# Which six weight tiles stay resident, and where one down tile stands in the last stages

## The chip, the cores and the metric

The kernel runs on one core of one Trainium2 chip. The metric is the device time of one execution in microseconds; three runs of the kernel before gave 2692.3, 2694.03 and 2695.58, with a median of 2694.03.

## The reference

Four sequences of 1024 tokens, 512 wide, go through two blocks, each of the form x = x + layernorm(block(layernorm(x))), all in float32.

```
proj = x @ W_in + b_in;  hidden, gate = split(proj)          # 512 -> 2 x 1024
conv = silu(causal depthwise conv of 4 taps (hidden))
dt_in, B, C = split(conv @ W_x);  delta = softplus(dt_in @ W_dt + b_dt)
h = exp(delta * A) * h + delta * conv * B;  y = sum_n h * C   # 16 states, over the tokens
block 1 = ((y + conv * d_param) * silu(gate)) @ W_out + b_out

x = fwht(x * SU_ug) / 64                                      # Hadamard transforms,
up, g = x @ W_up.T * s, x @ W_gate.T * s                      # folded into the weights by the kernel
block 2 = (fwht(silu(g) * up * SU_dp) / 64) @ W_down.T * s    # 512 -> 2048 -> 512
```

## The kernel before

The 4096 tokens are cut into NCH = 16 chunks of T = 256. The work is a pipeline of stages c = 0 to 18; each stage has 32 slots k. In stage c the scan runs for chunk c (`cur`), the input projection and the convolution for chunk c + 1 (`front`), the output projection of block 1 for chunk c - 1 (`back`), the feed-forward for chunk c - 2 (`ff`) and its remainder for chunk c - 3 (`fold`). Stages 16, 17 and 18 have no `cur` and no `front`: in stage 16 `back` is chunk 15, `ff` 14 and `fold` 13; in stage 17 `ff` is 15 and `fold` 14; in stage 18 only `fold` 15 is left. Each engine's instructions are written out slot by slot by its own function `slot`, and the engines meet in semaphores only.

The feed-forward of a chunk has HT = 16 tiles of 128 hidden units; tile ft of chunk j is number no = 16 j + ft. Each tile is `up_gate` (L686, 24 matmuls of 128x256: weights and activations are split into a high and a low part, three passes over each), then tanh on ScalarE, two products on VectorE, the split of the product into `prod_hi` (ScalarE) and `prod_lo` (GpSimd, `low`, L1356 on), and `down` (L707, 6 matmuls of 128x512, which add up in the two banks pD). In a stage, `up_gate(ff, ft)` stands in slot 2 + 2 ft and `down(ff, ft)` in slot 7 + 2 ft, up to ft = 12; down 13 and up_gate 15 stand in slot 0 of the next stage, down 14 in its slot 3, down 15 in its slot 5. In slot 1 `turn_f` transposes the feed-forward input of the next chunk into the bank hT; ScalarE and VectorE split it into fxT_hi and fxT_lo (`f_hi`, `f_low`), for which `up_gate(ff, 0)` waits. `turn_h` and `turn_y`, the transposes of the scan's last states and its sum, take the same bank after it. From chunk 14 on odd tiles use the bank `decay` in place of `pF`, as the scan is over.

The weights of one tile (1 MB for up and gate, `wug`; 0.5 MB for down, `wd`) are read again for each chunk into a ring of two buffers each. All DMAs are issued by SyncE in one program order. `load_ug` (L388) of a ring tile waits until the up_gate two ring tiles earlier is done, `load_wd` (L404) until the down two ring tiles earlier is. In slot k (odd) SyncE comes to the up and gate weights of tile (k + 1)/2, in slot k (even) to the down weights of tile (k - 4)/2; in slot 18, ahead of the down weights, `store_out` (L441) waits for the finished output of chunk c - 3, and in slot 20 `load_res` reads the residual rows.

When the scan is over its buffers hold six resident tiles, `kept_ug` and `kept_wd`: those of `KEPT` (L57). They are read once, in chunk 14 (`free_kept` waits until the scan's buffers are free), and used for chunks 14 and 15; `kept(no)` (L227) says which tile is resident, and `RINGED` numbers the others.

Of the kernel before, what the change touches and what calls it, by code (L numbers as in the profile page):

```python
# [19 lines left out]
NCH = TOK // T  # L20
# [6 lines left out]
def wait_first(eng, sem, value, passed):  # L27

    eng.wait_ge(sem, value)
    eng.sem_inc(passed, 1)  # L30


HT = FF // P


def fused_block(nc, x, W, scratch_bc, scratch_ug, scratch_wd, out):
# [17 lines left out]
        had_in1 = first("had_in1", [P, KT, DM])  # L54
        had_in2 = first("had_in2", [P, KT, DM])
    had_in = (had_in0, had_in1, had_in2)
    KEPT = range(2, 8)  # L57
    kept_ug, kept_wd = {}, {}
    with ExitStack() as once:
        once.enter_context(nc.sbuf_tensor("tail_pad0", [P, 8 * KT * T + 7 * T + 3 * TB * DM + TB * DI + DT * DM], F32))  # L60
# [7 lines left out]
    with ctx:  # L68
# [118 lines left out]
        for c in range(LAST + 1):  # L187
            cur, front, back, ff = chunk(c), chunk(c + 1), chunk(c - 1), chunk(c - 2)
# [38 lines left out]
        def kept(no):  # L227

            j, ft = divmod(no, HT)
            return ft - KEPT.start if j >= NCH - 2 and ft in KEPT else None  # L230

        RINGED = [no for no in range(NCH * HT) if kept(no) is None]
        RING_NO = {no: i for i, no in enumerate(RINGED)}
# [131 lines left out]
        def _(sp):  # L365
# [14 lines left out]
            def free_kept(i):  # L380

                wait_first(sp, y_gated, NCH - 1, sp_passed)
                if i in (1, 2, 3):
                    wait_first(sp, scan_done, NQ * NST * NCH, sp_passed)
                if i in (4, 5):
                    wait_first(sp, h_turned, TB * NST * NCH, sp_passed)

            def load_ug(j, ft):  # L388
                no = j * HT + ft
                if kept(no) is not None:  # L390
                    if j == NCH - 2:
                        free_kept(kept(no))
                        sp.dma_start(kept_ug[kept(no)][:, :, :, :].bitcast(F32), scratch_ug[ft, :, :, :].rearrange("p s (k m) -> p s k m", k=KT)
                                     ).then_inc(ug_kept[kept(no)], 16)
                    return
                i = RING_NO[no]
                if i >= 2:
                    wait_first(sp, ug_mm, RINGED[i - 2] + 1, sp_passed)
                if no == 0:
                    for part in ("r_hi", "r_lo"):  # L400
                        wait_first(sp, had_stored[part], 16 * SETS.count("r"), sp_passed)
                sp.dma_start(wug[i % 2][:, :, :, :].bitcast(F32), scratch_ug[ft, :, :, :].rearrange("p s (k m) -> p s k m", k=KT)).then_inc(ug_in[i % 2], 16)

            def load_wd(j, ft):  # L404
                no = j * HT + ft
                if kept(no) is not None:
                    if j == NCH - 2:
                        free_kept(kept(no))
                        sp.dma_start(kept_wd[kept(no)][:, :, :].bitcast(F32), scratch_wd[ft, :, :, :]).then_inc(wd_kept[kept(no)], 16)
                    return  # L410
                i = RING_NO[no]
                if i >= 2:
                    wait_first(sp, down_mm, RINGED[i - 2] + 1, sp_passed)
                if no == 0:
                    wait_first(sp, had_mm, NTILE, sp_passed)
                sp.dma_start(wd[i % 2][:, :, :].bitcast(F32), scratch_wd[ft, :, :, :]).then_inc(wd_in[i % 2], 16)
# [129 lines left out]
        def _(pe):  # L546
# [40 lines left out]
            def turn_f(j):  # L587
                pe.wait_ge(fn_done, TB * (j + 1))
                begin_t(("f", j, 0))
                for kt in range(KT):  # L590
                    for tb in range(TB):
                        mm = pe.transpose(hT[:, kt * T + tb * P:kt * T + (tb + 1) * P], ob[:, tb, kt * P:(kt + 1) * P], ident[:, :])
                mm.then_inc(fx_turned, 1)
# [92 lines left out]
            def up_gate(j, ft):  # L686
                no = j * HT + ft
                if kept(no) is None:
                    pe.wait_ge(ug_in[RING_NO[no] % 2], 16 * (RING_NO[no] // 2 + 1))
                else:  # L690
                    pe.wait_ge(ug_kept[kept(no)], 16)
                if ft == 0:
                    pe.wait_ge(fx_lo, 2 * (j + 1))
                if no:
                    pe.wait_ge(p_done, bank_users(no))
                else:
                    pe.wait_ge(had_lo, NTILE)
                if no == SPARE + 1:
                    pe.wait_ge(scan_done, NQ * NST * NCH)
                for which in (1, 0):  # L700
                    for kt in range(KT):
                        for i, (a, b) in enumerate(PASSES):
                            mm = pe.matmul(gate_up_bank(no)[:, which, :], ug_tile(no)[:, 2 * which + a, kt, :], fxT[b][:, kt, :],  # L703
                                           start=(kt == 0 and i == 0), stop=(kt == KT - 1 and i == len(PASSES) - 1))
                mm.then_inc(ug_mm, 1)

            def down(j, ft):  # L707
                no = j * HT + ft
                if kept(no) is None:
                    pe.wait_ge(wd_in[RING_NO[no] % 2], 16 * (RING_NO[no] // 2 + 1))  # L710
                else:
                    pe.wait_ge(wd_kept[kept(no)], 16)
                pe.wait_ge(p_lo, no + 1)
                if ft == 0 and j:
                    pe.wait_ge(z_evac, TB * j)
                split = (prod_hi[no % 2], prod_lo[no % 2])
                for tb in range(TB):
                    for i, (a, b) in enumerate(PASSES):
                        mm = pe.matmul(pD[tb][:, :], split[a][:, tb * P:(tb + 1) * P], wd_tile(no)[:, b, :],  # L719
                                       start=(ft == 0 and i == 0), stop=(ft == HT - 1 and i == len(PASSES) - 1))  # L720
                mm.then_inc(down_mm, 1)
# [27 lines left out]
            def in_slot(c, k, cur, front, back, ff, fold):  # L749
                n, tb = divmod(k, 2)  # L750
                if k == 0:
                    if front is not None:
                        turn_x(front)
                    if fold is not None:
                        down(fold, HT - 3)
                    if back is not None:
                        turn_h(back, NST - 1, 0)
                    if fold is not None:
                        up_gate(fold, HT - 1)
                    return  # L760
                if k == 1:
                    if ff is not None:
                        turn_f(ff)
                    if front is not None:
                        in_proj("hid", front, *PE_HID[0])
                    if back is not None:
                        turn_h(back, NST - 1, 1)
                    if front is not None:
                        in_proj("hid", front, *PE_HID[1])
                    return  # L770
                if k in (2, 3):
                    if back is not None:
                        turn_y(back, k - 2)
                    if ff is not None and k == 2:
                        up_gate(ff, 0)
                    if front is not None and k == 3:
                        in_proj("hid", front, *PE_HID[3])
                    if cur is not None:
                        turn_h(cur, 0, tb)
                    if front is not None and k == 2:  # L780
                        in_proj("hid", front, *PE_HID[2])
                    if fold is not None and k == 3:
                        down(fold, HT - 2)
                    return
                if cur is not None:
                    turn_h(cur, n - 1, tb)
                if ff is not None and k in UG_SLOT:
                    up_gate(ff, UG_SLOT[k])
                if front is not None and k in PE_HID:
                    in_proj("hid", front, *PE_HID[k])  # L790
                if back is not None:
                    out_proj(back, PE_OUT.get(k, ()))
                if cur is not None and k in PE_GATE:
                    in_proj("gate", cur, *PE_GATE[k])
                if front is not None:
                    x_proj(front, PE_XPROJ.get(k, ()))
                if ff is not None and k in DOWN_SLOT:
                    down(ff, DOWN_SLOT[k])
                if fold is not None and k in DOWN_LATE:
                    down(fold, DOWN_LATE[k])  # L800
                if front is not None:
                    if k == 23:
                        turn_rows(front)
                    if k in PE_DT:
                        dt_proj(front, PE_DT[k])
# [679 lines left out]
```

## Time and profile before

| | |
|---|---|
| median of three runs | 2694.03 us |
| the profiled execution, its own time | 2690.62 us |
| its span | 2688.8 us |
| TensorE busy | 2584.6 us (96%) |
| VectorE busy | 2239.1 us (83%) |
| GpSimd busy | 2046.8 us (76%) |
| ScalarE busy | 1818.1 us (68%) |
| DMA, mean over the span | 210 GB/s |

Times in the views are microseconds from the start of the span. Stage 16 begins at about 2493, stage 17 at about 2591, stage 18 at about 2669. In the view by stretches a line has the stretch, its length, then for PE, PEld, DVE, ACT and POOL the busy time and in brackets the count, then the granted clock (1.00 is 2.4 GHz), the DMA share and GB/s. In the chain of waits each line is start, duration, and what the chain ran through. "issue" is time in which the engine waited for nothing that the profile shows. L602, L610 and L592 are the transposes of turn_y, turn_h and turn_f, L703 is up_gate, L719 is down.

### The profile page before, as it was taken

Reading aid. Unit: us, or ns where it says so; the run is one execution under the profiler, and the core shown is the slowest. Engines: PE = TensorE matmul, PEld = TensorE weight load, DVE = VectorE, ACT = ScalarE, POOL = GpSimd, SP = SyncE. Lnnn points to the kernel's source line nnn. Section 1 sums busy time; section 2 is a strip of 40 time slices with the busy share of each in tenths; the row PEclk is TensorE's granted clock in tenths of the full one; section 3 lists DMA queues with packets and bytes.
Section 4 is the critical chain, followed back from the end, with each engine's and each line's share of the span. In section 5 each row is a group of like instructions: output and inputs, shape, how many; then the busy total and the mean of one; then the engine's idle time right before and its main releaser. Section 6 shows DMA issues by size and latency. Waiting matters only on the chain.

```text
span 2688.8 us, 46296 instructions
## 1 busy us (share of the span) xinstructions
PE 2584.6 (96%) x16048; PEld 2191.9 (82%) x16048; DVE 2239.1 (83%) x2567; ACT 1818.1 (68%) x3939; POOL 2046.8 (76%) x1692
## 2 busy tenths in 40 slices
PE   7899889999999999999999999999999999989987
PEld 5566568989888888988888888988888888878786
DVE  6698799898889889898889889898889888889321
ACT  4576677777777777777777777777777777755221
POOL 6576779788797979888797979888797979766222
PEclk9999999999999999999999999999999999999999
DMA  5554245766666665766666665766666665656564
GB/s 179 192 187 155 104 160 200 235 208 228 220 222 222 218 221 199 240 212 225 220 225 224 215 221 201 236 210 231 220 226 217 220 214 200 216 188 227 227 258 173
DMA packets 165193, 564.41 MB, mean 210 GB/s; under 512 B 17248, under 2 KB 19680, under 8 KB 132960
## 3 DMA queue, kind: packets, MB, share of 16 engines
q1 hardware_dynamic: 164960, 561.44, 60.5%
q8 instruction: 129, 2.11, 0.3%
q14 instruction: 104, 0.85, 0.1%
HBM read 527.30 MB, written 34.08 MB: 209 GB/s over the span
## 4 chain that ended last, share of the span: by engine, by line
PE 77%; DVE 10%; ACT 7%; issue 3%; DMA 2%; POOL 1%; SPq 0%; POOLq 0%; DVEq 0%; ACTq 0%
PE pF L703 21%; PE hT L610 13%; PE pM L628 13%; PE pD L719 10%; PE pM L680 8%; DVE h L1131 5%; DVE acc L1144 3%; PE pD L740 3%; PE pM L650 3%; PE decay L703 2%; PE hT L602 1%; ACT decay L952 1%; PE pF L740 1%; ACT delta L929 1%; ACT delta L924 1%
## 5 line engine op out<-in xcount | busy, mean ns | idle before, releaser
L1131 DVE TENSOR_TENSOR_SCAN h<-decay,dbx 128x512 f32<-128x512 f32 x1024 | 1201.2, 1206 | 97.6 <-ACT decay L952 68.1
L1299 POOL TENSOR_TENSOR dbx<-u,bb 128x2048 f32<-128x2048 f32 (+1 forms) x272 | 1179.1, 4335 | 37.7 <-DVE h L1131 35.7
L952 ACT ACTIVATE decay<-delta,a_neg 128x255 f32<-128x255 f32 x2048 | 875.5, 468 | 309.4 <-DVE h L1131 302.3
L703 PE MATMUL pF<-fxT_hi,wug 128*128 128x256 f32 x3744 | 735.2, 289 | 6.6 <-DMA wug<-scratch_ug 4.5
L1144 DVE SCALAR_TENSOR_TENSOR acc<-hT,bcT,acc 128x1024 f32<-128x1024 f32 x480 | 609.7, 1270 | 126.8 <-PE hT L610 123.4
L703 PEld LDWEIGHTS pF<-fxT_hi,wug 128*128 128x128 f32 x3744 | 604.1, 193 | 8.3 <-DMA wug<-scratch_ug 5.8
L610 PEld LDWEIGHTS hT<-ident,h 128*128 128x128 f32 x4096 | 472.3, 141 | 150.0 <-issue 96.9
L610 PE MATMUL hT<-ident,h 128*128 128x128 f32 x4096 | 534.6, 274 | 34.9 <-DVE acc L1144 22.5
L703 PE MATMUL pF<-fxT_lo,wug 128*128 128x256 f32 x1872 | 531.9, 284 | 0.0
L628 PE MATMUL pM<-xnT,w_in 128*128 128x256 f32 x2016 | 480.5, 381 | 10.6 <-ACT hid L872 4.9
L628 PEld LDWEIGHTS pM<-xnT,w_in 128*128 128x128 f32 x2016 | 366.2, 191 | 56.2 <-ACT hid L872 6.5
L1363 POOL TENSOR_TENSOR prod_lo<-prod,prod_hi 128x256 fp32r<-128x256 f32 x256 | 187.2, 731 | 293.0 <-ACT prod_hi L983 292.3
L703 PEld LDWEIGHTS pF<-fxT_lo,wug 128*128 128x128 f32 x1872 | 361.8, 193 | 0.2
L719 PE MATMUL pD<-wd,prod_hi 128*128 128x512 f32 x976 | 351.6, 441 | 3.8 <-POOL prod_lo L1363 2.0
L1356 POOL TENSOR_TENSOR conv<-conv,tap 128x256 f32<-128x256 f32 x360 | 261.3, 731 | 30.8 <-ACT tap L898 12.0
L680 PE MATMUL pM<-w_out,gate 128*128 128x512 f32 x512 | 240.4, 593 | 4.3 <-ACT hid L872 2.3
L719 PEld LDWEIGHTS pD<-wd,prod_hi 128*128 128x128 f32 x976 | 177.1, 190 | 59.6 <-issue 30.0
L719 PE MATMUL pD<-wd,prod_lo 128*128 128x512 f32 x488 | 192.8, 395 | 0.0
L976 ACT ACTIVATE th<-pF,half_gate 128x256 f32<-128x256 f32 x240 | 111.9, 466 | 107.1 <-PE pF L703 104.9
L898 ACT ACTIVATE tap<-hid,taps 128x256 f32<-128x256 f32 x360 | 155.6, 497 | 0.0
L1285 POOL COPY carry<-h 128x8 f32<-128x8 f32 x192 | 36.9, 192 | 149.3 <-issue 96.2
L1166 DVE SCALAR_TENSOR_TENSOR prod<-th,pF 128x256 f32<-128x256 f32 x240 | 98.7, 411 | 58.5 <-ACT th L976 58.5
(170 smaller groups left out, 2711.5 us busy)
## 6 DMA issues: line engine op xcount, KB each, us to landing
wug<-scratch_ug SPq DMA_DIRECT2D x244, 1024.0 KB, 4.8
wd<-scratch_wd SPq DMA_DIRECT2D x244, 512.0 KB, 4.0
w_in<-in_W_in SPq DMA_DIRECT2D x252, 256.0 KB, 2.9
bb<-scratch_bc SPq DMA_DIRECT2D x128, 256.0 KB, 4.7
xb<-in_hidden_states SPq DMA_DIRECT2D x16, 512.0 KB, 4.8
xr<-in_hidden_states SPq DMA_DIRECT2D x16, 512.0 KB, 6.0
out<-xr SPq DMA_DIRECT2D x16, 512.0 KB, 3.7
kept_ug<-scratch_ug SPq DMA_DIRECT2D x6, 1024.0 KB, 9.1
```

Of the source, the lines that this page charges most:

```text
L610: mm = pe.transpose(hT[:, dt * P:(dt + 1) * P], h[n % 2][:, dt, tb * P:(tb + 1) * P], ident[:, :])
L628: mm = pe.matmul(pM[:, a, :], w[:, kt, :], xnT[j % 2][:, kt, :], start=(kt == 0), stop=(kt == KT - 1))
L680: mm = pe.matmul(o, gate[:, dt, tb * P:(tb + 1) * P], w_out[:, dt, :], start=(dt == 0), stop=(dt == DT - 1))
L703: mm = pe.matmul(gate_up_bank(no)[:, which, :], ug_tile(no)[:, 2 * which + a, kt, :], fxT[b][:, kt, :], start=(kt == 0 and i == 0), stop=( ...
L719: mm = pe.matmul(pD[tb][:, :], split[a][:, tb * P:(tb + 1) * P], wd_tile(no)[:, b, :], start=(ft == 0 and i == 0), stop=(ft == HT - 1 and ...
L898: e = act.activation(tap[dt % 2][:, k, :], hid[:, dt, k:k + T], ACT.Copy, scale=taps[:, dt, k:k + 1])
L952: e = act.activation(da[q % 2][:, i, 1:], delta[c % 2][:, dt, 1:], ACT.Exp, scale=a_neg[:, dt, n:n + 1])
L1131: dve.tensor_tensor_scan(row(h[n % 2][:, tiles, :]), row(da[q % 2][:, :, :]), row(dbx[n % 2][:, tiles, :]), 0.0, ALU.mult, ALU.add).then_i ...
L1144: dve.scalar_tensor_tensor(acc[c % 2][:, tb, :], hT[:, :], cn, acc[c % 2][:, tb, :], ALU.mult, ALU.add).then_inc(acc_done, 1)
L1299: pool.tensor_tensor(dbx[n % 2][:, tiles, :], u[:, tiles, :], rows, ALU.mult).then_inc(done if restarts(c) else prod_done, 1)
L1356: pool.tensor_tensor(conv[j % 2][:, dt, :], conv[j % 2][:, dt, :], tap[dt % 2][:, k, :], ALU.add).then_inc(tap_added, 1)
L1363: pool.tensor_tensor(prod_lo[no % 2][:, :], prod[no % 2][:, :], prod_hi[no % 2][:, :].bitcast(F32), ALU.subtract).then_inc(p_lo, 1)
```

## The change

The resident tiles are 2, 4, 6, 8, 10 and 12 in place of 2 to 7. Tile 14 of chunk 15 is also read into a resident place, that of tile 2, after tile 2 of chunk 15 has been used (`second_use`); the semaphores of that place then count to 32. In stages without `cur` (16, 17, 18), `down(fold, 14)` is written out in slot 1, behind `turn_f`, in place of slot 3.

```
-    KEPT = range(2, 8)
+    KEPT = (2, 4, 6, 8, 10, 12)
         def kept(no):
             j, ft = divmod(no, HT)
-            return ft - KEPT.start if j >= NCH - 2 and ft in KEPT else None
+            if j >= NCH - 2 and ft in KEPT:
+                return KEPT.index(ft)
+            return 0 if second_use(no) else None
+
+        def second_use(no):
+            return no == HT * NCH - 2
+
+        FIRST_USE = HT * (NCH - 1) + KEPT[0]
             def load_ug(j, ft):
                 no = j * HT + ft
                 if kept(no) is not None:
-                    if j == NCH - 2:
+                    if second_use(no):
+                        wait_first(sp, ug_mm, FIRST_USE + 1, sp_passed)
+                    elif j == NCH - 2:
                         free_kept(kept(no))
+                    if second_use(no) or j == NCH - 2:
                         sp.dma_start(kept_ug[kept(no)] ...).then_inc(ug_kept[kept(no)], 16)
                     return
...
-                    pe.wait_ge(ug_kept[kept(no)], 16)
+                    pe.wait_ge(ug_kept[kept(no)], 32 if second_use(no) else 16)
...
                 if k == 1:
                     if ff is not None:
                         turn_f(ff)
+                    if cur is None and fold is not None:
+                        down(fold, HT - 2)
                     if front is not None:
                         in_proj("hid", front, *PE_HID[0])
...
-                    if fold is not None and k == 3:
+                    if cur is not None and fold is not None and k == 3:
                         down(fold, HT - 2)
```

`load_wd` and the wait in `down` change in the same way as `load_ug` and the wait in `up_gate`, with `down_mm` and `wd_kept`.

## Rows read from the trace of the kernel before

**Rows 1.** The page, busy time of TensorE, its share and its instructions.

```profile
PE 2584.6 (96%) x16048; PEld 2191.9 (82%) x16048; DVE 2239.1 (83%) x2567; ACT 1818.1 (68%) x3939; POOL 2046.8 (76%) x1692
```

**Rows 2.** Stretches of 5 us: five engines' busy time, granted clock, DMA share, GB/s.

```profile
2500.00:2505.00 5.00, 2.84 (x17) 2.64 (x18) 2.67 (x5) 0.58 (x2) 0.58 (x1) 0.75 1.02 429
2505.00:2510.00 5.00, 5.00 (x28) 5.00 (x28) 1.66 (x4) 0.04 (x1) 0.14 (x1) 0.57 0.13 54
...
2530.00:2535.00 5.00, 5.00 (x22) 3.01 (x21) 1.01 (x3) 0.47 (x1) 0.00 (x0) 1.00 1.03 425
...
2645.00:2650.00 5.00, 4.79 (x33) 4.14 (x32) 1.12 (x3) 0.89 (x2) 0.73 (x1) 1.00 0.88 329
```

**Rows 3.** Chain of waits, start of stage 16: start, duration, what it ran through.

```profile
2500.69 1.11 PE hT L610 x8
...
2503.25 1.94 PE hT L602 x8
2505.19 4.73 PE pF L703 x24
...
2510.80 1.38 PE pD L719 x6
```

**Rows 4.** TensorE in order of time, behind turn_f of stage 16; brackets: idle before.

```profile
2500.69 0.33 PE L610 MATMUL hT<-ident,h 128*128 128x128 f32 x1 [2.01 <-DVE fxT_lo L1158]
```

**Rows 5.** GpSimd in order of time: the low halves for the two moved down tiles.

```profile
2493.27 0.73 POOL L1363 TENSOR_TENSOR prod_lo<-prod,prod_hi 128x256 fp32r<-128x256 f32 x1 [5.65 <-ACT prod_hi L983]
...
2590.28 0.72 POOL L1363 TENSOR_TENSOR prod_lo<-prod,prod_hi 128x256 fp32r<-128x256 f32 x1 [5.40 <-ACT prod_hi L983]
```

**Rows 6.** Chain of waits, late stage 16 and early stage 17.

```profile
2559.97 2.89 PE decay L703 x24
...
2562.94 7.52 DMA wug<-scratch_ug
...
2583.64 7.52 DMA wd<-scratch_wd
...
2592.86 2.87 PE decay L703 x24
...
2596.60 2.06 issue
2598.66 3.11 PE pF L703 x24
...
2603.16 2.87 PE decay L703 x24
...
2607.42 2.87 PE pF L703 x24
```

**Rows 7.** SyncE in order of time: issues at the ends of its two long waits.

```profile
2522.58 0.42 SPq L402 DMA_DIRECT2D wug<-scratch_ug  x1
2555.25 0.39 SPq L444 DMA_DIRECT2D out<-xr  x1
...
2632.80 0.39 SPq L444 DMA_DIRECT2D out<-xr  x1
```

**Rows 8.** DMA issues at 2595.82, 2498.32 and 2522.58: count, KB each, us to landing.

```profile
wug<-scratch_ug SPq DMA_DIRECT2D x1, 1024.0 KB, 4.7
...
wd<-scratch_wd SPq DMA_DIRECT2D x1, 512.0 KB, 5.5
...
wug<-scratch_ug SPq DMA_DIRECT2D x1, 1024.0 KB, 20.8
```

**Rows 9.** Chain of waits, last tiles of stage 17.

```profile
2641.50 2.89 PE pF L703 x24
...
2654.56 7.60 DMA wug<-scratch_ug
...
2662.21 4.63 PE pF L703 x24
...
2669.59 2.89 PE decay L703 x24
```

More of the change, by code:

```diff
@@ L406, in load_wd @@
                 if kept(no) is not None:
-                    if j == NCH - 2:
+                    if second_use(no):
+                        wait_first(sp, down_mm, FIRST_USE + 1, sp_passed)
+                    elif j == NCH - 2:
                         free_kept(kept(no))
+                    if second_use(no) or j == NCH - 2:
                         sp.dma_start(kept_wd[kept(no)][:, :, :].bitcast(F32), scratch_wd[ft, :, :, :]).then_inc(wd_kept[kept(no)], 16)
@@ L711, in down @@
                 else:
-                    pe.wait_ge(wd_kept[kept(no)], 16)
+                    pe.wait_ge(wd_kept[kept(no)], 32 if second_use(no) else 16)
                 pe.wait_ge(p_lo, no + 1)
```

## The prediction

> **What bounds the kernel now.** I read the page first: TensorE is busy 96% of the span [rows 1], so only TensorE's own order and its idle time are worth anything, and the diff touches work in the last two hundred microseconds alone. There I read the stretches of 5 us, then the chain of waits, then SyncE's issues. The chain has three places for the reader.
>
> *The start of stage 16.* turn_f(14) ends at 2498.7, and TensorE then stands idle 2.01 us until VectorE has read the bank hT [rows 4]; another gap comes before turn_y, which starts at 2503.25 [rows 3]. TensorE is at its upper level (2.4 GHz) before, at 0.75 in 2500 to 2505 and at 0.57 in 2505 to 2510 [rows 2]: it fell to 1.2 GHz behind two gaps with one group of transposes between. The first feed-forward group there takes 4.73 us [rows 3] where the others take 2.87 [rows 6].
>
> *The late half of stage 16 and the last tiles of stage 17.* Here the chain runs through DMAs: up_gate(14,11) waits for a wug load, down(14,13) for a wd load, each 7.52 us after its issue [rows 6]; at the end a load of 7.60 us and a group of 4.63 [rows 9]. In the undisturbed part a tile (an up_gate and a down) comes every 4.26 us (2607.42 less 2603.16), of which up_gate is 2.87 and so down 1.39 [rows 6]. From up_gate(14,9) to up_gate(14,15) the chain takes 2592.86 - 2559.97 = 32.89 us; without waits it would be 5 x 4.26 + 2.87 + 2 x 1.39 = 26.95. **5.9 us are lost there.** From up_gate(15,10) to up_gate(15,15) it takes 2669.59 - 2641.50 = 28.09, without waits 4 x 4.26 + 5.65 = 22.69. **5.4 us are lost there**, 1.8 of them in the group of 4.63 us at half clock [rows 9].
>
> *Why the loads are late.* In a run of ring tiles, load i is issued when up_gate i-2 is done, so two tiles take a landing plus one up_gate: 7.5 + 2.9 = 10.4 us against the 8.5 that TensorE needs. A lone load lands in 4.7 us [rows 8]; it takes 7.5 because a wd load and the next wug load share the engines. And SyncE issues nothing between 2522.58 and 2555.25 and waits again before 2632.80 [rows 7]: both are the store of the feed-forward output, which sits in program order in slot 18.
>
> **The change part by part.**
>
> *down(f,14) behind turn_f, in stages 16 and 17.* Six matmuls, 1.39 us, move from the TensorE path (2510.80 in the chain, 1.38 [rows 3]) into the idle time behind turn_f: 2.01 us in stage 16 [rows 4], 2.06 in stage 17 [rows 6]. In stage 16 its low half is subtracted at 2493.27 to 2494.0 and in stage 17 at 2590.28 to 2591.0 [rows 5], before turn_f ends. Its weights in stage 16 are asked for before that, by a wait that the change leaves. It ends 0.6 us before hT comes free, so turn_h behind it is not delayed; if cover failed it would cost its 1.39 again, no more. The next in line at the old place, up_gate(.,1), waits for product 13,15 or 14,15, which VectorE has by then, as a whole up_gate(.,0) lies between. Nothing is queued behind the new wait that another engine needs sooner, and SyncE's load wd(14,0) is freed earlier. Gain 1.4 + 1.4 = **2.8 us**. In stage 18 the order is the old one, since turn_f is missing there and down(15,14) isn't moved ahead of anything.
>
> *The clock at 2502.* With down(13,14) in the first gap, TensorE has matmuls until 2500.1, idles 0.6, turns h, idles 1.5. At half clock turn_y cost 1.94 - 1.11 = 0.83 more and up_gate(14,0) 4.73 - 2.87 = 1.86 more [rows 3, 6]: 2.7 together. Bounds: 0 (it falls anyway) and 2.7, or a little more, as the gap of 2.06 at 2596.6 is filled too, where this profile had no fall but another execution may have. The nearest row is that one: a single gap of 2.06 between matmuls and 3.11 for the group behind it, not 4.73 [rows 6]. After the change the stretch is milder still. I take **2.7 us**.
>
> *Every other tile, stage 17.* Before, tiles 8 to 15 of chunk 15 come through the ring one after another; after, ring tiles are 0, 1, 3, 5, ... 13 and 15, so a ring load is issued two tiles and more ahead, some 10 us before its use against a landing of 4.7 to 7.6. Tile 14 is read into the place of tile 2, whose up_gate ends at 2610.3 [rows 6]; its load stands in order behind the loads of tile 13 and wd 11, issued some 12 us before up_gate(15,14). wd(15,15) waits for down(15,11), about 12 us ahead. After the store at 2632.80 the first down that needs a new load, down(15,7), is 7 us away, as before. So all of the **5.4 us** go, and with them the half clock at 2662, which stood behind a wait for a load. What is late next is nothing of the DMA: the closing chain tanh, product, high, low, down(15,15) stays.
>
> *Every other tile, stage 16.* Up to slot 18 SyncE issues the same loads as before (wug to tile 9, wd to tile 6), a few of them later: wug(14,3) now waits for up_gate(14,0), done 9 us before it is needed, wug 7 for up_gate 3, wug 9 for up_gate 5. These have slack, since out_proj stands between. After slot 18, wug 10, wd 8, wug 11, wd 9, wug 12 and wd 10 are now issued at once, not one by one. So the ring's round trip is gone and what bounds is the rate. From the store's issue (1.4 earlier than 2555.25) I lay the transfers behind one another in units of 512 KB: store, wd 7, wug 10 (2 units), residual, wd 8, wug 11, wd 9, wug 12, wd 10, wug 13, wd 11, wug 14, wd 12. Rate from the burst, 425 GB/s in 2530 to 2535 [rows 2], is 1.23 us a unit; from a ring stretch, 329 GB/s in 2645 to 2650, 1.59. The first lands some 3 us after its issue, an estimate below the 4.7 of a lone load of twice the size [rows 8].
> At 1.23 each tile lands before its use (wug 11 at about 2566 against 2566.9, wug 12 at 2570 against 2571, wug 13 at 2574 against 2575, wug 14 at 2578 against 2580). One wait is left: wd(14,13) is issued behind wug(14,15), which waits for up_gate(14,13). From there to down(14,13) are 1.39 + 2.87 + 1.39 = 5.65 us, and the pair needs 0.1 + 0.4 + 5.5 [rows 8], with 0.2 for the start: 0.6 late.
> At 1.59 the lateness is 1.1 at wug 11, about 0.5 at each of 12, 13 and 14, and 2.1 at wd 13: 4.7 in all.
> So the gain is between 5.9 - 4.7 = 1.2 and 5.9 - 0.6 = 5.3. The queue is deep here as in the burst, whose last load lands 20.8 us after issue for 16 units ahead of it [rows 8], so I stay near the fast end: 1.6 left, **4.3 us** gained.
>
> The Trainium skill (DMA: Bandwidth & Descriptors, Specifications) gives a core about 358 GB/s from HBM and 435 for the fabric. By the first figure a unit takes 1.47 us, an estimate, and the stage would keep some 2.2 us of waits; by the second it is my fast end. The trace has 425 GB/s of loads for 5 us [rows 2], so it doesn't agree with the first as a ceiling.
>
> **Sum.** 2.8 + 2.7 + 5.4 + 4.3 = 15.2 us. The profiled execution took 2690.62 (span 2688.8 and 1.8 around it), 3.4 below the median 2694.03. 2690.6 - 15.2 = 2675.4; against the median **2678.8 us**. From these four terms alone the time is 2675.0 to 2681 (1.0 more in stage 16 and one more fall of the clock spared, 1.8, at the low end).
>
> **The rivals.**
>
> *A. The clock falls all the same behind turn_f of stage 16.* For: between 2500.1 and 2504 there is still only a group of transposes between two gaps. Against: less idle than now, and no fall at 2596.6. All else holds: 12.5 gained, 2681.5.
>
> *B. The rate bounds stage 16.* For: the 329 GB/s, and the ring loads' landings don't follow the burst's pace. Against: with six transfers queued it is the burst's state. 2.8 + 1.2 + 5.4 with or without the clock: 9.4 to 12.1, 2682 to 2684.6.
>
> *C. It doesn't do what it says.* wd(14,14), which down(14,14) now needs at turn_f's end, is issued behind wug(15,0), 0.5 us behind the end of up_gate(14,14), and from there to turn_f's end are some 6.7 us. If both lag at the slow rate it is 3 late, the whole of stage 17 shifts by it, and with B little but the last 5.4 is left: 9.4 - 3 - 1.4 = 5, 2689. For: before, it landed as turn_f ended. Against: its own wait is now for down(14,11), not 12.
>
> *D. Slower, by the clock.* Place: any group after turn_f in stages 16 or 17. If TensorE fell to 1.2 GHz and stayed there, each up_gate costs 1.86 more and each down 1.4 more, 3.3 a tile. It decides from four tiles in a row (12.5 / 3.3); seven would give 2704. For: two falls in this stretch. Against: none outlasts two groups, all stand behind gaps, and the change only takes gaps away.
>
> **Chances.** Forecast 0.55, A 0.23, B 0.14, C 0.05, D 0.03. The range is from 2675.0 to 2684.6, which holds the forecast's case, A and nearly all of B. This kernel's measurement tells 0.2% (5.4 us) from no change. The forecast, A and B are faster by more: 0.92. C lies at the bound: 0.05 within. D: 0.03 slower.
>
> **What would show it.** In the trace after: down with wd directly behind the transposition of ob and TensorE idle some 0.6 before the next; the granted clock at 2500 to 2510 whole; from tile 9 of chunk 14 on a tile every 4.26 us, with one wait below 1 us at down(14,13); no DMA wait in stage 17 and no group over 3.2 us; wug issues at six within 6 us of the store. I am wrong if waits for wug of tiles 11 to 14 sum to over 3 us, if the moved down waits for its weights, or if the gain is under 9 us.

## The result, and the profile after

The changed kernel takes **2677.09 us** (median of six, 2674.68 to 2677.48) against 2692.61 for the kernel before (median of six, 2689.90 to 2695.58), 15.5 less. The ratio is 0.9942, 95% interval 0.9930 to 0.9954. The forecast was 2678.8, with a range of 2675.0 to 2684.6.

The profiled execution took 2677.31 (span 2675.5) against 2690.62. Its line numbers are shifted: turn_f is L606, turn_y L616, turn_h L624, up_gate L717, down L733.

The chain of waits at the start of stage 16, to be laid beside [rows 3]:

```profile
2501.30 1.11 PE hT L624 x8
...
2503.86 1.06 PE hT L616 x8
2504.93 2.88 PE pF L717 x24
2507.80 0.87 PE hT L616 x8
2508.68 2.88 PE decay L717 x24
2511.55 1.39 PE pD L733 x6
2512.94 2.87 PE pF L717 x24
```

turn_y takes 1.06 in place of 1.94 and up_gate(14,0) 2.88 in place of 4.73; the down between turn_y and up_gate(14,1) is gone. The stretches of 5 us, with the granted clock in the third column from the end, against [rows 2]:

```profile
2500.00:2505.00 5.00, 2.91 (x21) 2.22 (x21) 3.31 (x6) 1.19 (x3) 0.00 (x0) 1.00 0.96 401
2505.00:2510.00 5.00, 5.00 (x45) 5.00 (x44) 2.91 (x8) 2.13 (x3) 0.74 (x1) 1.00 0.73 254
```

TensorE's idle times from there to stage 17, in order of time (idle before and its end in brackets), against [rows 4]:

```profile
2501.30 1.09 PE L624 MATMUL hT<-ident,h 128*128 128x128 f32 x8 [0.62 <-DVE fxT_lo L1174]
...
2564.04 0.73 PE L733 MATMUL pD<-kept_wd,prod_hi 128*128 128x512 f32 x2 [0.43 <-DMA kept_wd<-scratch_wd]
...
2566.54 0.39 PE L717 MATMUL decay<-fxT_hi,wug 128*128 128x256 f32 x1 [0.83 <-DMA wug<-scratch_ug]
...
2584.72 0.73 PE L733 MATMUL pD<-wd,prod_hi 128*128 128x512 f32 x2 [0.87 <-DMA wd<-scratch_wd]
...
2592.17 0.36 PE L717 MATMUL pF<-fxT_hi,wug 128*128 128x256 f32 x1 [0.41 <-issue]
```

The chain from late stage 16 to the end, which answers to [rows 6, 9]:

```profile
2578.72 5.95 DMA wd<-scratch_wd
...
2584.72 1.66 PE pD L733 x6
2586.38 2.86 PE decay L717 x24
2589.24 0.87 PE hT L606 x8
2590.11 1.65 PE pD L733 x6
2591.76 0.41 issue
2592.17 3.11 PE pF L717 x24
2595.28 2.88 PE decay L717 x24
...
2599.55 2.87 PE pF L717 x24
...
2656.29 2.89 PE decay L717 x24
```

No DMA stands in stage 17 any more: from up_gate(15,2) at 2599.55 to up_gate(15,15) at 2656.29 there are 56.74 us, against 62.17 before (2607.42 to 2669.59). The loads have their lead: the last one for the ring, wug(15,15), is issued at 2640.85 and lands at 2645.4, 10.9 us ahead of its use; before it was issued at 2658.89 and landed at 2666.2, 3.4 us ahead, and wug(15,14) landed at 2662.2 for a group that starts at 2662.21.

**Where the time of the two profiles went.** Four pieces are bounded by instructions that all kernels have: the twelve matmuls of down(13,12) and down(13,13), up_gate(14,2), up_gate(14,15), up_gate(15,2), up_gate(15,15), the end. All traces of the study, in us; the pieces are read from the chain of waits, and in no_second_use and early_store, where the chain passes by a bound, from TensorE in order of time:

| trace | to up(14,2) | to up(14,15) | to up(15,2) | to up(15,15) | from the first to the end |
|---|---|---|---|---|---|
| before | 25.15 | 76.43 | 14.56 | 62.17 | 197.52 |
| before_again_a | 24.98 | 75.01 | 16.01 | 64.90 | 200.41 |
| before_again_b | 24.98 | 74.96 | 16.02 | 61.35 | 196.54 |
| after | 21.05 | 73.44 | 13.17 | 56.74 | 183.61 |
| changed_again | 21.05 | 72.19 | 13.16 | 56.75 | 182.39 |
| changed_third | 21.04 | 72.98 | 13.18 | 56.74 | 183.17 |
| down_only | 21.03 | 75.76 | 13.20 | 62.99 | 192.97 |
| tiles_only | 24.97 | 73.10 | 14.57 | 56.74 | 188.61 |
| gap_filled | 22.78 | 75.01 | 14.90 | 62.85 | 194.83 |
| no_second_use | 21.04 | 72.38 | 13.16 | 57.48 | 183.27 |
| residual_later | 21.03 | 72.21 | 13.19 | 56.74 | 182.41 |
| early_store | 21.03 | 71.31 | 13.19 | 56.74 | 181.55 |
| early_store_wd_first | 21.03 | 70.46 | 13.18 | 56.74 | 180.68 |
| best_again | 21.03 | 70.46 | 13.19 | 56.74 | 180.64 |

The mean from there to the end is 198.16 for the three traces of before and 183.06 for the three of the changed kernel: 15.1 less. What lies ahead is the same work in all and yet not the same time: the twelve matmuls start between 2488.19 and 2493.89. A single pair of spans is worth no more than that. The pieces agree far better, apart from the fourth in the kernel before, which goes from 61.35 to 64.90.

### The profile page after: what moved, and what is told of

It is laid out like the page before. It is cut to its first block, busy times and chain, and to the rows that moved or that the text cites. A ratio compares the mean times of both kernels' runs of the same rounds, so it can differ in the third digit from the quotient of the medians.

```text
span 2675.5 us, 46296 instructions
## 1 busy us (share of the span) xinstructions
PE 2581.3 (96%) x16048; PEld 2190.1 (82%) x16048; DVE 2238.6 (84%) x2567; ACT 1818.1 (68%) x3939; POOL 2046.8 (77%) x1692
## 4 chain that ended last, share of the span: by engine, by line
PE 77%; DVE 10%; ACT 8%; issue 3%; DMA 1%; POOL 1%; SPq 0%; POOLq 0%; DVEq 0%; ACTq 0%
PE pF L717 21%; PE hT L624 14%; PE pM L642 13%; PE pD L733 10%; PE pM L694 8%; DVE h L1147 5%; DVE acc L1160 3%; PE pD L754 3%; PE pM L664 3%; PE decay L717 2%; ACT decay L968 1%; PE hT L616 1%; PE pF L754 1%; ACT delta L945 1%; ACT delta L940 1%
## 5 line engine op out<-in xcount | busy, mean ns | idle before, releaser
L717 PE MATMUL pF<-fxT_hi,wug 128*128 128x256 f32 x3632 | 710.2, 289 | 0.4 <-issue 0.4
L624 PEld LDWEIGHTS hT<-ident,h 128*128 128x128 f32 x4096 | 472.8, 141 | 148.5 <-issue 96.7
L717 PEld LDWEIGHTS pF<-fxT_hi,wug 128*128 128x128 f32 x3632 | 583.6, 192 | 0.9 <-issue 0.8
L624 PE MATMUL hT<-ident,h 128*128 128x128 f32 x4096 | 535.2, 274 | 33.6 <-DVE acc L1160 22.5
L717 PE MATMUL pF<-fxT_lo,wug 128*128 128x256 f32 x1816 | 514.8, 283 | 0.0
L733 PE MATMUL pD<-wd,prod_hi 128*128 128x512 f32 x972 | 350.8, 442 | 2.8 <-POOL prod_lo L1379 2.0
L717 PEld LDWEIGHTS pF<-fxT_lo,wug 128*128 128x128 f32 x1816 | 349.8, 193 | 0.0
L733 PEld LDWEIGHTS pD<-wd,prod_hi 128*128 128x128 f32 x972 | 176.7, 190 | 58.9 <-issue 30.5
L733 PE MATMUL pD<-wd,prod_lo 128*128 128x512 f32 x486 | 192.0, 395 | 0.0
L694 PEld LDWEIGHTS pM<-w_out,gate 128*128 128x128 f32 x512 | 88.3, 191 | 67.8 <-issue 63.1
```

The costliest lines, as they stand in the source:

```text
L624: mm = pe.transpose(hT[:, dt * P:(dt + 1) * P], h[n % 2][:, dt, tb * P:(tb + 1) * P], ident[:, :])
L694: mm = pe.matmul(o, gate[:, dt, tb * P:(tb + 1) * P], w_out[:, dt, :], start=(dt == 0), stop=(dt == DT - 1))
```

## The experiments

All were timed beside the kernel before on their chip, whose medians were 2691.3 (24 executions, first four kernels), 2689.0 (9, next four) and 2689.8 (9, last four).

**down_only**: the moved down alone.

```
     KEPT = range(2, 8)                      # as before
+                    if cur is None and fold is not None:
+                        down(fold, HT - 2)  # slot 1, behind turn_f
```

> Only the moved down tile (13,14 and 14,14 behind turn_f); resident tiles 2 to 7 as before. Theory: it gives 2 x 1.4 us of TensorE time and 2.7 us of spared half clock at the start of stage 16, so 5.5 us below the kernel before; the waits for ring loads in late stage 16 (5.9 us) and stage 17 (5.4 us) stay, since each ring load is issued by TensorE's own progress and so shifts with it. Rival 1 (the clock at 2502 is a matter of the execution, not of the filled gap): 2.8 us. Rival 2 (the ring stretches swallow what is gained ahead of them): under 2 us.

Median 2686.10, ratio 0.9979 (0.9970 to 0.9988), so 5.2 us by the medians, as the theory has it. The first piece is 4.1 us shorter, the third 1.4. Both rivals fall: without the clock the first piece would have stayed at 23.6 to 23.8, and the stretches of the ring swallow nothing that the traces could tell: they have 75.76 and 62.99, within what the three traces of before show. Stage 17 keeps its waits.

**tiles_only**: the alternating tiles alone.

```
     KEPT = (2, 4, 6, 8, 10, 12)             # as in the changed kernel
-                    if cur is None and fold is not None:
-                        down(fold, HT - 2)
-                    if cur is not None and fold is not None and k == 3:
+                    if fold is not None and k == 3:
                         down(fold, HT - 2)
```

> Only the alternating resident tiles and the second use of tile 2's place; the down tile stays in slot 3. Theory: stage 17 gives 5.4 us, late stage 16 some 3.0 as in the changed kernel, so 8.4 us below the kernel before, 5.5 above the changed kernel; the half clock at the start of stage 16 stays. Rival (the parts help each other: with the down in its old place the loads behind the store of slot 18 are relatively earlier or later): stage 16 differs from the changed kernel by more than 1 us.

Median 2682.11, ratio 0.9971 (0.9960 to 0.9981), 9.2 us by the medians. Stage 17 has its 56.74, late stage 16 lies among the changed kernel's three (73.10), and the first piece and the third are those of before, with the half clock. The two gains add up to 14.4 by the medians, against the 15.5 of the whole change; by the traces' last column they are 5.2 and 9.6, 14.7 together, against 15.1. So the parts don't help or hinder each other by more than about 1 us, which is as fine as these runs can tell.

**no_second_use**: tile 14 of chunk 15 in the ring.

```
         def second_use(no):
-            return no == HT * NCH - 2
+            return False
```

> The changed kernel with tile 14 of chunk 15 in the ring instead of in tile 2's place. Theory: the second use is worth nothing: wug(15,15) would wait for up_gate(15,13), from whose end to up_gate(15,15) there are 1.39 + 2.87 + 1.39 + 1.39 = 7.0 us against a landing of 4.7 to 6, so within 0.5 us of the changed kernel. Rival (three ring tiles in a row at the end are enough for a late load, as the traces before show landings of 7.5 us): 1 to 3 us slower than the changed kernel, with a wait for wug or wd in the last 12 us of TensorE.

Median 2674.97, ratio 0.9948 (0.9935 to 0.9961): not told apart from the changed kernel. The trace shows the small wait that the theory denied, TensorE in order of time:

```profile
2653.44 0.73 PE L733 MATMUL pD<-wd,prod_hi 128*128 128x512 f32 x2 [0.45 <-DMA wd<-scratch_wd]
```

It is down(15,13), late behind its load by 0.45, 0.7 with the slower start, and stage 17 has 57.48 us in the table against 56.74. So the second use, with most of the diff's lines, brings 0.7 us of the 15 in this one trace: more than the 0.5 of the theory, less than the rival's 1 to 3.

**gap_filled**: nothing moved, the gap filled with idle work.

```
                     if ff is not None:
                         turn_f(ff)
+                    if c == LAST - 2:
+                        spare = da[1][:, :, :].rearrange("p a t -> p (a t)")
+                        for _ in range(3):
+                            pe.matmul(spare, ident[:, :], w_out[:, 0, :], start=True, stop=True)
```

> The kernel before with three 128x512 matmuls of constant data, whose result nobody reads, behind turn_f of stage 16; nothing is moved. They take some 1.3 us of the 2.0 us gap. Theory (the gap lets the clock fall, filling it keeps it up): the clock stays whole from 2500 to 2510, up_gate(14,0) takes 2.9 us, gain 2.7 us. Rival 1 (the fall is chance): fall in the profile and a gain within 0.5 us of zero. Rival 2 (the fall only moves to another place): no gain, with half clock elsewhere in stage 16.

Median 2688.50, 2.8 below the kernel before by the medians, but the ratio is 0.9995 (0.9986 to 1.0004), which allows for no gain as well as for the 2.7 expected: the executions alone don't decide it. The chain of waits does:

```profile
2499.19 0.87 PE hT L592 x8
2500.06 2.58 PE decay L767 x6
2502.64 0.89 PE hT L610 x8
...
2504.99 1.06 PE hT L602 x8
2506.05 2.88 PE pF L703 x24
```

The spare matmuls took 2.58 us, not the 1.3 expected, and held turn_h back by some 0.6. Even so the first piece is 22.78 against 24.97 to 25.15 in the four traces with the empty gap: 2.2 to 2.4 won with work that computes nothing. turn_y and up_gate(14,0) have the times of full clock, and there is no half clock in the rest of stage 16. Rivals 1 and 2 fell, as far as one trace can tell; the traces that follow say the same of rival 1.

**before_again_a**, **before_again_b**: the kernel before, for its trace.

> The kernel before once more, for its trace. Theory (the empty 2.0 us behind turn_f of stage 16 bring the clock down): half clock from about 2502 to 2509 again, up_gate(14,0) at 4.5 us or more, as in the two traces with the empty gap so far, against none of the seven traces where the gap is filled. Rival (chance): full clock there. The part up to stage 16 will differ by up to 2.5 us from the first trace, with the places of half clock before 400 us.

> As before_again_a. Half clock near 2502 again. The fall at 2662 is expected only if the waits for wug at tiles 13 and 14 of chunk 15 fall as in the first trace; over the traces the length from stage 16's start to the end is 196 to 199 us.

One execution each, 2696.11 and 2692.21 us. Half clock is there both times (stretches of before_again_a, the granted clock third from the end):

```profile
2500.00:2505.00 5.00, 2.38 (x20) 1.90 (x18) 1.86 (x3) 1.45 (x3) 0.00 (x0) 0.97 0.63 235
2505.00:2510.00 5.00, 4.14 (x20) 4.17 (x21) 3.12 (x7) 0.42 (x1) 0.72 (x1) 0.50 0.69 289
2595.00:2600.00 5.00, 2.94 (x26) 2.74 (x25) 1.69 (x4) 1.45 (x3) 0.00 (x0) 1.00 0.64 217
2600.00:2605.00 5.00, 5.00 (x28) 4.86 (x27) 0.55 (x2) 0.89 (x2) 0.73 (x1) 0.66 0.42 175
```

So it fell in all four traces with the empty gap of stage 16 (before three times, tiles_only) and in none of the ten with the filled one (eight when the expectation above was written, not seven). The last row was not expected: it falls behind turn_f of stage 17 too, where [rows 6] show 3.11 for the same up_gate(15,0). The chain of before_again_a there:

```profile
2599.67 4.60 PE pF L703 x24
```

before_again_b has the same 4.60. The third piece is 16.0 there, not 14.6: what the moved down saves in stage 17 is then 1.4 and 1.45 of clock. before_again_a had a fall at 2671 as well and 64.90 us in stage 17. Its length to the end, 200.41, lies outside the 196 to 199 expected. But the same gap of 2.06 behind turn_f of stage 17 is also in tiles_only and gap_filled, and there the clock held: it fell in two of five traces with that gap empty, and in none of the nine in which the moved down fills it.

**changed_again**, **changed_third**: the changed kernel itself.

> The changed kernel itself, beside the next three on one chip. It should stand 13.3 to 15.5 us below the kernel before, with 2.9 to 3.0 us of waits and restarts left between up_gate(14,9) and up_gate(14,15).

> The changed kernel, third trace, beside the next kernel: from the two downs ahead of stage 16 to the end 182.4 to 183.6 us, as in the two traces so far; 1.7 to 3.0 us of it waits for loads in stage 16.

Medians 2677.06 and 2676.34, ratios 0.9951 (0.9937 to 0.9966) and 0.9941 (0.9929 to 0.9954). By the medians that is 11.9 and 13.5 below the kernel before on the same chip, against 15.5 in the result: the first lies under the 13.3 expected, and the nine executions of before beside it spread over 10.6 us. Above the 70.46 that up_gate(14,2) to up_gate(14,15) takes without any wait, the three traces have 3.0, 1.7 (changed_again, where 2.9 to 3.0 were expected) and 2.5.

**residual_later**: the residual rows behind wug(14,11).

```
-                if k == 20 and back is not None:
+                if k == 20 and cur is not None and back is not None:
                     load_res(back)
...
                         load_ug(j, ft % HT)
+                    if k == 21 and cur is None and back is not None:
+                        load_res(back)
```

> The changed kernel with the residual rows of chunk 15 asked for behind wug(14,11) (slot 21) in place of ahead of wd(14,8) (slot 20), in stage 16 and after alone. Theory (the waits of 0.4 us at down(14,8) and 0.8 at up_gate(14,11) are the residual's place in the queue: it and the 2.9 us until the next landing, where others take 1.3): both waits vanish, about 1.7 us faster than the changed kernel with their restarts, and the slow landing stands behind wug 11. Rival (the slow landing belongs to the start of the burst behind the store, whatever comes first): wd 8 is still late, gain at most 0.8 us.

Median 2676.18, ratio 0.9947 (0.9932 to 0.9962), 0.9 below the changed kernel on the same chip: no gain that the times can tell. The waits at down(14,8) and up_gate(14,11) are gone, but the piece is 72.21 as against 72.19 in changed_again, since down(14,13) waits longer, TensorE in order of time:

```profile
2579.78 0.73 PE L735 MATMUL pD<-wd,prod_hi 128*128 128x512 f32 x2 [1.13 <-DMA wd<-scratch_wd]
```

That wait is 0.87, 0.64 and 1.25 in the three traces of the changed kernel, so its length here may be chance. And my reason falls: with nothing of the residual ahead of it, wug(14,11) still landed 3.5 us after its forerunner (2560.4 against 2556.9) where two units take 2.5. The slow landing comes within the first transfers behind the store, whichever they are. The rival has that right, but not that wd 8 would still be late.

**early_store**: the data of the store are ready earlier.

```
                 if n == 9:
...
-                    if fold is not None:
+                    if fold is not None and cur is not None:
                         add_z(fold)
+                if n == 6 and fold is not None and cur is None:
+                    add_z(fold)
```

> The changed kernel with GpSimd's addition of the feed-forward output to the residual (add_z) in slot 12 in place of slot 18, in stages without scan; SyncE's store of slot 18 then finds its data ready. Theory (SyncE stands behind the store for no need; the memory moves 0 GB/s from 2540 to 2550): the store and the loads behind it go out some 15 us earlier, no wait for wug or wd is left but that of down(14,13), some 1.8 us faster than the changed kernel. Rival (the late half is bound by the rate): waits at tiles 11 to 14 stay.

Median 2674.95, ratio 0.9945 (0.9929 to 0.9962). The store goes out at 2535.73 in place of 2551.76, and a tile comes every 4.26 us from 2547.71 on. What waits is down(14,13), 0.56 us, and, 0.20, the moved down(14,14). It is 2.1 us below the changed kernel by the medians and 1.5 by the last column of the table, against 1.8 expected. The rate did not bind: the rival fell. The early store was not tried on the kernel before, so what it would have done for the ring loads without the alternating tiles isn't known.

**early_store_wd_first** and **best_again**: also the last two loads of stage 16 exchanged.

```
+                    if c == NCH and k == 29:
+                        load_wd(j, HT - 3)
                     if j is not None:
                         load_ug(j, ft % HT)
...
-                    if j is not None:
+                    if j is not None and not (c == NCH and k == 30):
                         load_wd(j, ft % HT)
```

> early_store and, in stage 16, wd(14,13) asked for ahead of wug(14,15), for which SyncE waits until up_gate(14,13) is done. Theory (the remaining 0.9 us wait, 1.1 with its restart, is that order alone): the wait at down(14,13) goes, no DMA is left in the chain of stage 16, 2.9 us faster than the changed kernel. Rival (wug(14,15) becomes late in its place): a wait of 0.5 to 1 us at up_gate(14,15), and no more than early_store brings.

> early_store_wd_first again. Theory: no DMA in the chain from stage 16 on, the same 180.7 us from there to the end, 1.7 to 2.9 below the changed kernel of this call; in the time of the executions 2 us, at the edge of what the runs can tell. Rival (the first trace was a lucky one): a wait for wug or wd returns.

Medians 2674.86 and 2674.41, ratios 0.9943 (0.9929 to 0.9957) and 0.9937 (0.9923 to 0.9950). No DMA stands in the chain from stage 16 on. Late stage 16 of best_again:

```profile
2577.83 2.87 PE pF L719 x24
2580.71 2.75 PE pD L735 x12
2583.45 2.87 PE decay L719 x24
```

down(14,12) and down(14,13) run as twelve matmuls without a gap, and up_gate(14,15) follows. The two traces take 180.68 and 180.64 to the end, 2.4 below the changed kernel's mean. The medians lie 2.2 and 1.9 below the changed kernel's on the same chips; the intervals of the ratios overlap, so the trace shows this gain and the times only agree with it.

## Why the prediction was right

*The moved down, 2.8.* Right. Six matmuls stand behind turn_f, idle 0.62 is left in stage 16 and 0.41 in stage 17, up_gate(14,1) directly follows turn_y, and the third piece is 1.4 shorter. Its weights in stage 17 came at the last moment: issued at 2582.98 and 7.1 us on the way, they landed at 2590.1, as turn_f ended. The gap behind it hid the slow start (1.65 for 1.39). That was rival C's place, and the margin was as thin as I feared: in early_store and no_second_use this down waited for its weights by 0.20 and 0.22.

*The clock at 2502, 2.7.* Right in place and size. First piece: 4.0 shorter, of which 1.39 is the down, so 2.6 for the clock. gap_filled shows it apart from any moved work. Rival A gets none of ten traces. What I held against it, that a single gap of 2.06 leaves the clock whole at 2596.6 [rows 6], holds only in part: it did so in three of five traces, and the other two fell.

*Stage 17, 5.4.* Right, 5.43 between these traces; from the other two traces of before it is 8.2 and 4.6, so the fit of the one number owes something to the trace it was worked out from. But the second use of tile 2's place, to which I gave a paragraph, has 0.7 of it; the alternation does the rest.

*Late stage 16, 4.3, with 1.6 us of waits left.* **This term was mis-sized.** The profiles have 73.44 against 76.43, 3.0 gained; over three traces of each, 72.9 against 75.5, 2.6 gained and 2.4 left. The wait at down(14,13), forecast 0.6 with its start, was 0.87 and its 0.26, of the kind foreseen: early_store keeps it and the exchange of the two loads removes it. The step that was off is "one wait is left": there are three in this trace, 0.43 at down(14,8), 0.83 at up_gate(14,11) and that one. The first two come from the landings at the front of the queue. DMA issues of the changed kernel at 2551.76, 2556.17 and 2570.28 (count, KB each, us to landing):

```profile
out<-xr SPq DMA_DIRECT2D x1, 512.0 KB, 3.3
...
wug<-scratch_ug SPq DMA_DIRECT2D x1, 1024.0 KB, 10.3
...
kept_wd<-scratch_wd SPq DMA_DIRECT2D x1, 512.0 KB, 8.7
```

From the store's landing at 2555.1 to wug(14,11)'s at 2566.5 seven units of 512 KB came in 11.4 us, 1.63 each; from there to wd(14,12)'s at 2579.0 ten in 12.5, 1.25 each. I had taken 1.23 for all of them. So the landings of the first tiles came at the slow end of my bounds (1.59) and the rest at the fast one, which is why the waits are at tile 8 and tile 11 and nowhere behind. But the reason that I gave for the slow end, a rate of 329 GB/s, was not there. The stretches between these landings (granted clock, DMA share and GB/s at the end):

```profile
2555.10:2566.50 11.40, 10.17 (x66) 8.84 (x65) 2.53 (x6) 3.97 (x8) 4.19 (x5) 1.00 1.02 403
2566.50:2579.00 12.50, 12.46 (x89) 11.77 (x90) 3.40 (x9) 2.27 (x5) 3.25 (x7) 1.00 0.81 330
```

In the first, 4.60 MB moved at 403 GB/s, but the seven units that landed hold 3.67; in the second, 4.13 MB moved and the ten units that landed hold 5.24. So by the landing of wug(14,11) the engines had also moved at least 0.9 MB of loads asked for later, and my sum, which lays each transfer behind the one before, is wrong at the front of a burst. Rival B has the lateness for the first third of the stretch, not its cause. Why the engines are that far ahead there stays open: residual_later excludes the residual rows, and the store itself was not left out.

*The sum.* The forecast gain was 15.2 and the medians have 15.5, but that they agree so well is in part luck. Between the two profiled executions the four pieces of the table come to 4.1 + 1.4 + 5.4 + 3.0 = 13.9 and the executions differ by 13.3. One error hid another: in the first trace the waits cost 1.4 more than forecast, and the trace on which I worked lacked the half clock at 2600 that two others had (1.45). I had allowed for it as "one more fall of the clock spared" at the low end of the range. So the 3.4 us by which that execution lay below its median were probably such falls in part; the changed kernel's profiled execution lies at its median.

The Trainium skill (DMA: Bandwidth & Descriptors, Specifications) gives some 358 GB/s as the limit of one core from HBM. This trace doesn't agree with it as a ceiling: it has 424 GB/s in 2520 to 2525 and in 2525 to 2530, and 403 where the loads were late.

## What to carry to other kernels

Where a buffer ring of two is late only for want of lead, buffers that are resident already bring more if they are spread among the ring's tiles than in a row: every ring load between two of them then has more lead, at no cost in memory. Work moved into an idle gap of TensorE may be worth its own time and again as much in clock; look what the granted clock does behind the gap, in more than one trace. And before the rate is blamed, look for what the issuing queue itself stands behind: here a store waited in order for an addition that could have been done 16 us earlier.

## What was not expected of the hardware

- The clock falls behind a gap of 2.06 us between TensorE's groups in some executions and not in others: at 2600 in two of five traces with that gap empty. At 2502, where a gap of 2.01 and a second one of 1.47 have a group of transposes between them, it fell in four of four.
- A load can be late while the memory moves 403 GB/s, as at least 0.9 MB of the loads behind it had moved when wug(14,11) landed.
- Three matmuls of 128x512 in plain float32 appear as six and take 2.58 us, 0.86 for each of mine; the six of a down, in the format of the split weights, take 1.39.
- Work that is the same in all kernels and untouched by the edits, up to 2488, varied by 5.7 us between 14 traces; the stretches of half clock before 400 us sit at different places (at 136 or 274, at 294 or 314), and residual_later, which has none there, starts the twelve matmuls first.
